# Splitting the down product in a gated unit's step, moving one cast, and two products ahead of an expert stage

## What is computed

```python
x = x + jnp.tanh(g_xattn[0]) * _L0_xattn_ref(_layernorm(x), token_ids, ctx, ctx, ctx)       # 4 experts picked by token id
x = x + jnp.tanh(g_ffn[0]) * _L0_ffn_ref(_layernorm(x), w_gate, w_up, w_down)               # the gated unit
x = x + jnp.tanh(g_xattn[1]) * _L1_xattn_ref(_layernorm(x), ctx, ctx, gamma)                # 8 heads
x = x + jnp.tanh(g_ffn[1]) * _L1_ffn_ref(_layernorm(x), gate_w, bias, ...)                  # 64 experts, 6 per token, and a shared one

def _L0_ffn_ref(x, w_gate, w_up, w_down):      # x: 2048 rows of 512; 2048 hidden columns
    gate = _mx_linear(x, w_gate)               # _mx_linear quantizes both operands: blocks of 32 share
    up = _mx_linear(x, w_up)                   # an exponent (that of the block's largest magnitude)
    inter = jax.nn.silu(gate) * up
    return _mx_linear(inter, w_down)
```

## Time and profile before

| what | value |
|---|---|
| three executions | 1055.09, 1054.49, 1052.22 us; median 1054.49 |
| the profiled execution | 1057.53 us, its span 1055.6 us |
| mean granted TensorE clock | 0.97 of 2.4 GHz |
| PE busy | 963.0 us, 91% of the span |
| DVE, ACT, POOL busy | 656.9 (62%), 397.2 (38%), 638.1 us (60%) |
| the chain that ended last | PE 56%, POOL 17%, DVE 14%, issue 8% |

### The profile page before, as it was taken

The page is one execution under the profiler, slowest core; times in us unless marked ns, Lnnn a source line. Parts: engine busy times, 40 slices in busy tenths (PEclk is TensorE's granted clock), DMA queues, the critical chain, the costliest instruction groups (busy, mean ns, idle before and its releaser), DMA issues.

```text
span 1055.6 us, 13607 instructions
## 1 busy us (share of the span) xinstructions
PE 963.0 (91%) x4398; PEld 469.5 (44%) x4398; DVE 656.9 (62%) x1208; ACT 397.2 (38%) x801; POOL 638.1 (60%) x562
## 2 busy tenths in 40 slices
PE   4979999659999999799999999989999999999992
PEld 3445554324444444344444445325555555555530
DVE  6679887968888887677777777981222222222221
ACT  4434445324444444466666665331111111111100
POOL 4497887548788887686767671245444554445430
PEclk9989999869999999999999999998999999999997
DMA  7655555240000000230001605168999999999648
GB/s 260 238 122 138 124 127 135 36 159 1 1 2 1 1 2 19 84 148 21 22 21 35 235 1 200 31 257 281 339 345 347 347 343 342 336 342 341 149 73 171
DMA packets 64147, 162.89 MB, mean 154 GB/s; under 512 B 9888, under 2 KB 10032, under 8 KB 63632
## 3 DMA queue, kind: packets, MB, share of 16 engines
q1 hardware_dynamic: 47488, 116.94, 31.5%
q0 software_dynamic: 16464, 40.91, 17.8%
q10 hardware_dynamic: 128, 4.19, 1.1%
HBM read 129.67 MB, written 39.67 MB: 160 GB/s over the span
## 4 chain that ended last, share of the span: by engine, by line
PE 56%; POOL 17%; DVE 14%; issue 8%; ACT 2%; DMA 1%; ACTq 0%; POOLq 0%; DVEq 0%
PE PS L1568 16%; PE PS L1587 8%; PE PS L1413 6%; PE PS L1390 6%; PE PS L1401 6%; POOL ARENA L657 6%; POOL ARENA L663 3%; PE PS L1557 3%; PE PS L364 3%; DVE ARENA L985 2%; POOL XNT L600 2%; POOL ARENA L652 2%; DVE ARENA L890 2%; PE PS L1310 1%; DVE ARENA L1194 1%
## 5 line engine op out<-in xcount | busy, mean ns | idle before, releaser
L707 POOL TENSOR_TENSOR ARENA<-ARENA 128x512 f32<-128x512 f32 x128 | 133.2, 1061 | 54.5 <-DVE ARENA L1020 54.4
L1356 PE MATMUL PS<-SLAB,ARENA 128*128 128x512 bf16 x512 | 119.5, 385 | 6.7 <-DVE ARENA L971 4.6
L753 POOL DMA_INDIRECT out<-ARENA,idx x32 | 45.9, 1436 | 127.4 <-DVE ARENA L1226 122.5
L1831 ACT ACTIVATE ARENA<-PS 96x192 f32<-96x192 f32 x64 | 20.9, 326 | 228.8 <-PE PS L1568 183.7
L1226 DVE COPY ARENA<-PS 96x512 f32<-96x512 f32 x64 | 41.1, 682 | 94.1 <-PE PS L1587 94.1
L1738 ACT ACTIVATE ARENA<-PS,ARENA 128x512 f32<-128x512 f32 x128 | 86.7, 682 | 23.4 <-DVE ARENA L1014 20.1
L1568 PE MATMUL PS<-SLAB,ARENA 128*96 128x384 f32 x240 | 83.4, 501 | 0.0
L1014 DVE TENSOR_REDUCE ARENA<-PS 128x2 f32<-128x1024 f32 x64 | 78.2, 1222 | 7.2 <-PE PS L1390 6.9
L1356 PEld LDWEIGHTS PS<-SLAB,ARENA 128*128 128x128 bf16 x512 | 49.1, 99 | 69.1 <-issue 15.0
L1401 PEld LDWEIGHTS PS<-ident,ARENA 128*128 128x128 f32 x512 | 54.8, 141 | 51.1 <-issue 35.0
L1704 ACT ACTIVATE ARENA<-PS 128x512 f32<-128x512 f32 x64 | 38.2, 597 | 104.4 <-PE PS L1356 85.8
(11 more groups left out here) (263 smaller groups left out, 1835.2 us busy)
## 6 DMA issues: line engine op xcount, KB each, us to landing
SLAB<-in_L_ffn_w_gate SPq DMA_DIRECT2D x30, 384.0 KB
SLAB<-in_L_ffn_w_up SPq DMA_DIRECT2D x30, 384.0 KB
X<-in_L_ffn_w_down SPq DMA_DIRECT2D x14, 768.0 KB
SLAB<-in_L_ffn_w_down SPq DMA_DIRECT2D x10, 768.0 KB
CT<-in_L_ffn_w_gate SPq DMA_DIRECT2D x16, 384.0 KB
CT<-in_L_ffn_w_up SPq DMA_DIRECT2D x16, 384.0 KB
X<-in_ctx SPq DMA_DIRECT2D x4, 1024.0 KB, 5.6
XNT<-in_L_ffn_w_gate SPq DMA_DIRECT2D x16, 256.0 KB
```

Of the source, the lines that this page charges most:

```text
L707: last = pool.tensor_tensor(prob[s % 4][:, h, :], prob[s % 4][:, h, :], rec[:, s % 4, h:h + 1].to_broadcast([P, D]), ALU.mult)
L1356: last = pe.matmul(bank(b), QT[:, par, k * P:(k + 1) * P], w[:, k, c * D:(c + 1) * D], start=(k == 0), stop=(k == KD - 1))
```

## The change

In the gated unit the down product of tile i-1 is cut into two halves of 8 matmuls; the first is issued between chunks 2 and 3 of tile i, the second at the end of the step. Both transposes come between chunk 2 and chunk 3. ACT's order follows (`it(i-1, 1)` and `qt(i+1)` ahead of the fourth SiLU), and on DVE `cast_h(i+2)` goes ahead of `product_i(i, 3)`. In front of S6 a wait is taken out of `turn_rows` and stands once ahead of two products into bank 0 that nothing reads.

```diff
@@ DVE, step(i, par) @@
                     if live(i, 0):
                         cast_i(i, 0)
+                    if live(i, 2):
+                        cast_h(i + 2)
+                    if live(i, 0):
                         product_i(i, 3, par)
                         measure_i(i, 1, par)
-                    if live(i, 2):
-                        cast_h(i + 2)
@@ PE @@
-                def down(i):
-                    need(pe, x2_ready, i)
-                    for h in range(2):
-                        pe.wait_ge(it_out, i * 2 + (h + 1))
-                        for k in range(KI // 2 * h, KI // 2 * (h + 1)):
-                            last = pe.matmul(bank(7), IT[:, k * P:(k + 1) * P], WDT[:, k, :], start=(k == 0), stop=(k == KI - 1))
-                    last.then_inc(down_done, 1)
+                def down_half(i, h):
+                    if h == 0:
+                        need(pe, x2_ready, i)
+                    pe.wait_ge(it_out, i * 2 + (h + 1))
+                    for k in range(KI // 2 * h, KI // 2 * (h + 1)):
+                        last = pe.matmul(bank(7), IT[:, k * P:(k + 1) * P], WDT[:, k, :], start=(k == 0), stop=(k == KI - 1))
+                    if h == 1:
+                        last.then_inc(down_done, 1)
@@ PE, step(i, par) @@
                     if live(i, 0):
                         gate_up(i, 2, par)
-                        gate_up(i, 3, par)
                     if live(i, -1):
+                        down_half(i - 1, 0)
                         turn_i(i - 1, 1, 1 - par)
                     if live(i, 1):
                         turn_q(i + 1, 1 - par)
+                    if live(i, 0):
+                        gate_up(i, 3, par)
                     if i == NT - 1:
                         scores(0)
                     if live(i, -1):
-                        down(i - 1)
+                        down_half(i - 1, 1)
@@ PE, behind the last step @@
-                down(NT - 1)
+                down_half(NT - 1, 0)
+                down_half(NT - 1, 1)
@@ PE, S6 @@
                 def turn_rows(e):
                     pe.wait_ge(g_in6[e % GR], 16 * (e // GR) + 16)
                     need(pe, bt_out, e - 1)
-                    if e < 2:
-                        pe.wait_ge(ub_ready, up_count(GCH - 2, 0))
...
+                pe.wait_ge(ub_ready, up_count(GCH - 2, 0))
+                for n in range(2):
+                    pe.matmul(bank(0), ident[:, :], XG[:, GCH - 1, 0, :], start=True, stop=True)
                 turn_rows(0)
                 turn_rows(1)
@@ ACT, step(i, par) @@
                     if live(i, 0):
                         silu_g(i, 2)
-                        silu_g(i, 3)
+                    if live(i, -1):
+                        it(i - 1, 1)
                     if live(i, 1):
                         qt(i + 1, 1 - par)
-                    if live(i, -1):
-                        it(i - 1, 1)
+                    if live(i, 0):
+                        silu_g(i, 3)
```

## The result

| | before | after |
|---|---|---|
| median of four executions each | 1053.36 us | 1063.02 us |
| range | 1051.29 to 1055.09 | 1062.66 to 1063.12 |
| the profiled execution, its span | 1057.53, 1055.6 | 1063.09, 1061.3 |
| mean granted clock | 0.970 | 0.968 |

The ratio is 1.0086, 95% interval 1.0069 to 1.0102: slower by 9.1 us (7.3 to 10.8); the two medians of the table lie 9.7 us apart. The forecast was 1063.5 us.

A forecast was written before the change was run, and what follows sets the result against it. The prediction took a gapless DVE-POOL loop in the gated unit as the bound, PE close behind. The unit's 10.9 us more minus S6's 1.95 gave 9.0, set on the 1054.5 us median: 1063.5 us, whole range 1057 to 1070.

The forecast's parts named there:

- The bound: Gated unit's steady steps: a gapless loop of DVE and POOL sets their length, with PE only 0.23 us behind.
- DVE-POOL ring: Gated unit: loop of casts, measurements and normal_i on DVE and POOL; steps of 12.68 and 13.22 us become 13.02 and 13.56.
- ScalarE's order: Gated unit: the fourth SiLU, now behind it(i-1, 1) and qt(i+1), stays hidden by 1 us.
- The new wait: Ahead of down's first half: PE stalls 1.77 us for leave(i-2), replacing 0.57 us of removed waits a step.
- PE's ring: Gated unit: new loop of cast, leave, PE's work, product and next cast, taking 13.28 us a step.
- The moved cast: Gated unit: cast_h(i+2) ahead of product_i(i, 3) adds 0.34 us to the loop of DVE and POOL.
- collision rival: Gated unit: back_i goes ahead of cast_h, which waits out its 1.91 us; 22 us more, 1085 us; 6 in 100.
- The sum of the unit: Whole gated unit: 4.7 + 0.7 + 2.3 + 3.2 = 10.9 us more.
- C(12) to C(15): Gated unit from cast_i(11, 1) to cast_i(14, 1), without enter: 37.53 us becomes 39.84, 2.3 us more.
- Last step: Step 15: scores(0) waits for tile 15's fourth SiLU, delaying largest(0) and cast_i(15, 0); 3.2 us added.
- The clock at the unit's end: End of gated unit: longer PE idling could lower its clock, 0 to 3 us more, taken as 0.
- S6's front: Ahead of the first expert: two products of 0.4 to 0.6 us keep PE's clock full; 1.95 us less.

The follow-up runs named there:

- cast_only: The kernel before with only cast_h(i+2) moved ahead of product_i(i, 3): 1.0037 of the kernel before.
- pe_order_freed: The changed kernel with the cast back, PE waiting for leave's first instruction and the last step in old order; S6 part kept: 1.0003 of the kernel before.
- early_bank7: The changed kernel with PE's first half of down waiting for leave's first instruction instead of its last: 1.0048 of the kernel before.
- s6_only: The kernel before with only the S6 part, two unread products and no wait in turn_rows: 1.0000 of the kernel before.
- cast_back: The changed kernel with cast_h(i+2) back behind measure_i(i, 1): 1.0066 of the kernel before.
- last_step_old: The changed kernel with, in step 15, the fourth gate and up chunk and its SiLU ahead of down's first half again: 1.0060 of the kernel before.
- before_b: The kernel before, unchanged, run again for a second trace: 1052.88 us.
- before_c: The kernel before, unchanged, run again for a third trace: 1053.75 us.

## Why the prediction was right, step by step

**The bound.** Right for the steps up to the eleventh. The DVE-POOL ring set them, and PE was 0.2 us behind. cast_only and pe_order_freed show it: one instruction more in that ring lengthens every step up to the eleventh, and PE's new order, with a stall no longer than its old waits, changes none of these steps by more than 0.02 us. What the prediction did not see is that from step 12 on, without `enter`, the ring runs through `back_i` and PE's transposes, so there the waits ahead of the transposes are on the way. It did no harm to the forecast, which took these steps as measured (37.53 us). Of their removal pe_order_freed shows 0.10 us in three steps.

**ScalarE's order.** Forecast as hidden, and it was: pe_order_freed keeps it in steps 1 to 14 and loses nothing there.

**The new wait.** Right in place and size: 1.75 us behind `bn_aggr` (1.77 forecast). early_bank7 shows that it is this signal.

**PE's ring.** 13.10 us, forecast 13.28. DVE's signal took 0.06 us, not 0.14, and from the next PE group to the cast 1.43, not 1.51. PE's ring sets eight steps (one of each pair, and steps 12 to 14), so each 0.1 us counts eight times.

**The moved cast.** Mechanism right, size too large: 0.22 us net, not 0.34. It delays the measurement by 0.33, but `normal_i(i, 1)` starts alone now and takes 1.91 us instead of 2.02. The prediction had both durations in the earlier trace rows and used the longer one for the collision rival only. What it missed: the moved cast also moves `normal_i` and the power operation behind it, which makes step 13 0.69 us longer. In the changed kernel leave's wait sets that step, and this shows only in cast_only and early_bank7. The rival that `back_i` goes first did not occur: it took 2.03 us, the cast 0.41.

The Trainium skill (SBUF — State Buffer, Who interferes with whom) says that, of a DVE operation in a two-port mode and one of GpSimd, the one that issues first holds the ports to SBUF that the two share for its whole length. The traces agree where DVE was first: its casts, ahead by 0.16 us (342.68) and 0.10 us (395.87 in cast_only), kept their length, and POOL's operations grew by 0.12 and 0.45 us. They do not agree in step 13 of the kernel before, where POOL's small power operation was first by 0.14 us and DVE's cast kept its 0.69 us: there the order of the starts did not decide.

**The sum of the unit.** 8.5 us, forecast 10.9. Steps 0 and 1: 0.54 (0.7). Five pairs: 3.27 (4.7). C(12) to C(15): 1.77 (2.3). Last step: 2.95 (3.2). Taken out one at a time of the changed kernel, the cast gives back 1.66, the early signal 2.83, the last step 2.55, 7.0 in sum. All three together give back 8.15: with one of them gone, another still holds some of the steps.

**The clock at the unit's end.** Forecast 0 of 0 to 3: from the last cast to the first gather 276.97 and 276.68, so 0.

**S6's front.** The weakest step. In the profiled pair the gain was 1.85 (forecast 1.95), but timed alone the part is worth 0 (within about 2 us either way). The products were mis-sized: forecast 0.4 to 0.6 each, measured 1.0, and the trace of before had the same 1.94 us for two products of that size (its shared products at 707.66). So the first rows are 1 us late where the shared products run at the lower clock. That by itself did not lengthen the front: the changed kernel's trace has this lateness and 12.07 us.

What the prediction had right is that the third gather then sets the front; what it took as fixed is how long that gather takes. From its issue to PE's start on its rows (forecast 3.5 us) it is 3.45 and 3.47 in after and early_bank7, but 4.40, 4.16, 4.35 and 4.62 in s6_only, cast_back, pe_order_freed and last_step_old. The third expert's product starts 3.59 us behind that in every one of them but last_step_old, whose second expert ran at the lower clock. Why the gather takes longer in some executions no run here shows. Six traces with two products have fronts of 12.07 to 14.93 us, mean 13.0; five without 13.05 to 13.98, mean 13.7. So 0.7 us on average, which no run here can resolve.

**The total.** 1063.5 against 1063.02 us. The mechanism of the unit was right, but that the total agrees to 0.5 us is in part luck. Two errors cancel in part: the unit's loss was put 2.4 us too high, S6's gain some 1.3 to 2 us too high. Taking the sum as a difference and setting it on the median was needed too: from the profiled execution the sum says 1066.5, and the profile after has 1063.09. Of these 3.4 us the unit is 2.4, and 1.2 lie at the end of the span, which the forecast had as unchanged; the other stretches together take 0.2 back.

**What stays open.** Why the third gather takes 3.3 us in some executions and up to 4.6 in others. Why the stages ahead of the unit take 3 us more in some executions. Whether the 1.7 us by which one added product shortens the front reach the end: in the traces about 2 us do, in the timed runs it is neither shown nor excluded.

## What to carry to other kernels

Before moving work into an engine's idle time, find the ring that sets the step. If the engine is not in it, filling its waits wins nothing, and a moved instruction brings its own wait along: look where its release stands in the other engine's order, here 1.75 us behind the new place, and at what is queued behind it. At the end of a loop, check each consumer that expected the moved work to be long over; the last step alone cost 2.95 us of 8.5.

## What the runs showed of the hardware

A gap of PE of the same length can keep the full clock or lose it. One of 2.28 us at the program's end kept it in the trace of before (granted clock 1.00) and lost it in that after (granted clock 0.50 from 1037.7 on):

```profile
1030.80 1.96 PE L1505 MATMUL PS<-ARENA 128*128 128x512 f32 x4 [2.28 <-DVE ARENA L1245]
1037.64 3.65 PE L1510 MATMUL PS<-ARENA 128*128 128x512 f32 x4 [2.28 <-DVE ARENA L1246]
```

The gap of 1.87 us ahead of the lists' transposes, which stand before the shared products in S6's front, lost it in before_b (2.90 us for these products) and not in before_c (1.94). The prediction's argument that a 2.28 us gap had kept it was therefore weak evidence. One f32 product of 128x512 takes 1.0 us at the full clock in these traces.
